# Moving a shared on-chip arena from a start of 32 modulo 128 bytes to a multiple of 128 bytes

## The reference, cut to what matters

```python
# layer 0: 32 query heads of 16, 8 key/value heads, then a residual sum and a layer norm with gamma, beta
x = norm(softmax(q @ k.T / 4 + mask) @ v @ Wo + bo + x) * gamma + beta
# layers 1 and 2: 16 heads of 128 over the same context, one extra key and value (bias_k, bias_v) per head
for i in (1, 2):
    h = layer_norm(x) * scale_i + offset_i
    q, k, v = h @ wq_i + bq_i, ctx @ wk_i + bk_i, ctx @ wv_i + bv_i
    x = x + softmax(q @ [k, bias_k].T / sqrt(128)) @ [v, bias_v] @ wo_i + bo_i
# MLP: width 2048, exact gelu
h = layer_norm(x) * scale + offset
x = x + gelu(h @ w_fc1 + b_fc1) @ w_fc2 + b_fc2
```

## Time and profile before

| what | value |
|---|---|
| time, median of 3 runs | 2512.69 us (2512.53 to 2516.67) |
| the profiled execution: its own time | 2512.67 us |
| its span, first to last instruction | 2510.9 us |
| matmuls busy (PE) | 2395.5 us, 95% of the span |
| weight loads busy (PEld) | 2045.5 us, 81% |
| VectorE, ScalarE, GpSimd busy | 1240.8, 862.7, 807.9 us |
| mean granted TensorE clock | 0.987 |

### The profile page before, as it was taken

One profiled execution on the slowest core, in us unless ns is written; L12 is line 12 of the kernel. 1 busy time (PEld: TensorE's weight loads), 2 busy tenths in 40 slices (PEclk: granted clock), 3 DMA queues, 4 the chain that ended last, 5 costly groups with the idle time before them and its releaser, 6 DMA issues.

```text
span 2510.9 us, 40711 instructions
## 1 busy us (share of the span) xinstructions
PE 2395.5 (95%) x14896; PEld 2045.5 (81%) x14896; DVE 1240.8 (49%) x2038; ACT 862.7 (34%) x2484; POOL 807.9 (32%) x584
## 2 busy tenths in 40 slices
PE   6898999999999999999979889999999999998999
PEld 5677888888888888777766778888888888887777
DVE  6985333434433333465579853333354333334654
ACT  5964222223322222332259642222233222223311
POOL 4964222233322223210059542223243222323100
PEclk9999999999999999999989999999999999999999
DMA  5002001111000101011140020111110010110110
GB/s 200 10 10 80 34 33 58 35 57 56 35 34 33 42 33 54 18 43 58 67 165 10 10 80 34 42 50 42 50 55 34 34 42 33 42 50 14 59 42 34
DMA packets 34545, 120.16 MB, mean 48 GB/s; under 512 B 3456, under 2 KB 3712, under 8 KB 33408
## 3 DMA queue, kind: packets, MB, share of 16 engines
q1 hardware_dynamic: 34432, 118.69, 13.1%
HBM read 114.48 MB, written 4.19 MB: 47 GB/s over the span
## 4 chain that ended last, share of the span: by engine, by line
PE 84%; DVE 6%; issue 4%; ACT 3%; POOL 3%; DMA 0%; DVEq 0%; SPq 0%; ACTq 0%; POOLq 0%
PE PS L504 71%; PE PS L691 4%; PE PS L707 4%; PE PS L699 2%; POOL XN L367 1%; ACT PS L1008 1%; DVE XN L1203 1%; PE PS L572 1%; ACT AT L1008 1%; DVE MX L1208 1%; PE PS L682 1%; DVE X L1227 1%; POOL P0D L367 0%; DVE SUM L1213 0%; DVE XN L1285 0%
## 5 line engine op out<-in xcount | busy, mean ns | idle before, releaser
L504 PE MATMUL PS<-AT,W 128*128 128x512 f32 x2496 | 606.8, 393 | 10.8 <-DVE AT L1295 10.7
L504 PEld LDWEIGHTS PS<-AT,W 128*128 128x128 f32 x2496 | 468.4, 189 | 117.0 <-DVE AT L1295 18.0
L429 POOL TENSOR_TENSOR PR<-PR,RC 128x512 f32<-128x512 f32 x128 | 133.3, 1041 | 984.3 <-DVE RC L1372 984.3
L1227 DVE TENSOR_TENSOR X<-PS,X 128x512 f32<-128x512 f32 x416 | 286.1, 689 | 312.0 <-PE PS L504 306.9
L504 PE MATMUL PS<-CT,W 128*128 128x512 f32 x1584 | 403.3, 404 | 29.8 <-DVE W L334 25.0
L504 PE MATMUL PS<-W,CX 128*128 128x512 f32 x1632 | 403.7, 401 | 7.6 <-DVE Q L1195 3.1
L504 PE MATMUL PS<-W,CT 128*128 128x256 f32 (+1 forms) x3264 | 406.7, 284 | 0.0
L504 PEld LDWEIGHTS PS<-W,CT 128*128 128x128 f32 x3264 | 394.8, 191 | 1.6 <-issue 0.8
L504 PEld LDWEIGHTS PS<-CT,W 128*128 128x128 f32 x1584 | 293.2, 191 | 90.1 <-DVE W L334 25.5
L504 PEld LDWEIGHTS PS<-W,CX 128*128 128x128 f32 x1632 | 300.3, 188 | 80.0 <-DVE Q L1195 4.3
L1039 ACT ACTIVATE CX<-PS,VEC 128x512 fp32r<-128x512 f32 x128 | 88.1, 688 | 672.4 <-PE PS L707 672.4
(11 more groups left out here) (109 smaller groups left out, 2452.0 us busy)
## 6 DMA issues: line engine op xcount, KB each, us to landing
RAW<-in_wq SPq DMA_DIRECT2D x44, 512.0 KB, 4.4
RAW<-in_wo SPq DMA_DIRECT2D x44, 512.0 KB, 3.2
RAW<-in_wk SPq DMA_DIRECT2D x40, 512.0 KB, 3.2
RAW<-in_wv SPq DMA_DIRECT2D x40, 512.0 KB, 3.7
X<-in_x SPq DMA_DIRECT2D x2, 2048.0 KB, 9.0
BVR<-in_bv_rows SPq DMA_DIRECT2D x8, 512.0 KB, 3.8
out<-X SPq DMA_DIRECT2D x4, 1024.0 KB, 4.2
BIASVR<-in_biasv_rows SPq DMA_DIRECT2D x6, 512.0 KB, 5.0
```

The costliest lines, as they stand in the source:

```text
L429: nc.gpsimd.tensor_tensor(PR[:, :, 0:P], PR[:, :, 0:P], RC[:, 0, 0:BT].unsqueeze(2).to_broadcast([P, BT, P]), ALU.mult).then_inc(norm_done, 1)
L504: ins = nc.tensor.matmul(out, lhs(c, a), rhs(c, b), start=(k == 0), stop=(k == total - 1))
L1227: V_.tensor_tensor(X[:, tile, :], PS[:, bank, :], X[:, tile, :], ALU.add).then_inc(done, 1)
```

## The change

```diff
         ARENA = 61440
-        at = (nc.sbuf_base + 31) // 32 * 32
-        sb("arena", [P, ARENA // 4])
+        at = (nc.sbuf_base + 127) // 128 * 128
+        sb("arena", [P, ARENA // 4 + 24])
```

## The result

| | before | changed |
|---|---|---|
| median of 20 runs | 2514.23 us (2512.53 to 2516.67) | 2507.02 us (2503.72 to 2512.64) |
| ratio, 95% interval | | 0.9974 (0.9967 to 0.9981) |
| profiled execution, its span | 2512.67, 2510.9 us | 2507.58, 2505.8 us |
| mean granted clock of the profiled run | 0.987 | 0.985 |

The change makes the kernel 0.26% faster, 7.2 us between the medians and 5.1 us between the two profiled spans. The forecast was no change, 2512.7 us, with 0.15 for faster. The time lies inside the stated range, the direction was missed.

The account below looks back on a forecast made before the run. The prediction took the matrix engine to bound the kernel, with the large products at 71% of the span. Span 2510.9 us plus 1.8 us around it plus 0 for every term gave 2512.7 us, range 2500 to 2518 us.

Parts of the forecast that it names:

- the 0 for the pace of the 512-wide streams out of the arena: Matrix engine, HB and CX streams: the new starts change their pace by nothing, 0 us.
- a price of 17.3 us: HB and CX streams: gain if the residue causes all their slowness, 4.7 us plus 12.6 us; kept as one end.
- Weight loads and transposes show no cost: Matrix engine: loads take 188 ns from the arena, 189 from W; transposes 1.03 us per eight at either residue.
- Keys with both tiles at a multiple of 128 run at two paces: Keys stream, CT moving and W stationary: 237.2 and 228.1 ns at the same addresses, so pace depends on what ran before.
- The 128-wide products run alike in and out of the arena: Attention's small products: 110.5 ns outside the arena, 110.6 and 112.0 inside, so no gain from these 2048 matmuls.
- a nanosecond of a stream in the MLP is one of the kernel: MLP: the matrix engine is busy for all of 100 us, so each nanosecond per matmul counts in the kernel's time.
- Rival A: HB and CX streams: stationary operand at residue 32 or 96 costs, 0 or 64 does not; 17.3 us gain, 2495.4 us, chance 0.14.
- Its variant with 2508.0 us: Only a start at 0 counts, not 64: CX of layers 1 and 2 stays slow, little more than HB's 4.7 us left.
- Rival B: Matrix engine: two operands starting at the same residue get in each other's way; 8.4 us slower, 2521.1 us, chance 0.06.
- VectorE, ScalarE, GpSimd and the transfer were costed at 0: Other engines' arena tiles: 0, bounds -0.3 us and 0; ROWV's transfer: 0, with 128 us of slack.
- The 3 beats: ROWV's transfer: its new address wastes 3 more beats of 32 bytes on 4096 bytes, an estimated 2% of the transfer.

Follow-up runs that it names:

- e1: The kernel before with HB alone moved from residue 32 to 0 modulo 128: 2512.83 us, ratio 0.9997 to the kernel before.
- e2: The kernel before with CX of layers 1 and 2 alone moved by 32 bytes, from residue 96 to 0: 2513.99 us, ratio 1.0006.
- f1: e3 with the whole arena another 128 bytes up: 2509.58 us, ratio 0.9984 to the kernel before.
- f2: e3 with 128 bytes of padding ahead of W, moving W and all behind it: 2519.26 us, ratio 1.0022 to the kernel before.
- f4: e3 with 32 bytes of padding ahead of W and the arena another 32 up: 2519.04 us, ratio 1.0019 to the kernel before.
- h1: e3 plus four PSUM banks for the second MLP product, with AT moved 128 bytes and W and all behind it 256: 2510.64 us, ratio 0.9988 to before.
- e4: The changed kernel with HB put back to residue 32 and CX to 96: 2516.86 us, ratio 1.0014 to the kernel before.
- e3: The changed kernel with PT and CX another 64 bytes up, so every arena tile starts at a multiple of 128: 2506.42 us, ratio 0.9971 to before.

## Why the prediction was wrong

The failing step is the one named in it: the 0 for the pace of the 512-wide streams out of the arena. The rows had shown the two slow streams, 6.1 and 7.7 ns slower, and a price of 17.3 us. The runs showed CX 5.5 ns a matmul faster and 6.4 us in all, and HB 7.3 ns faster while it does not wait. I argued it away with three comparisons, and each was of something else.

- *Weight loads and transposes show no cost.* True, and they still show none: HB's loads take 188 ns before and in e1. But what differs is the step from one pair of load and matmul to the next. The transposes are 128 columns wide and use IDENT as moving tile, so they have another pair of starts.
- *Keys with both tiles at a multiple of 128 run at two paces.* The 237.2 ns hold the first step after a float32 product, 0.31 us. Inside the same stream without it, in a timeline of the kernel before,

```profile
801.58 1.55 PE L504 MATMUL PS<-CT,W 128*128 128x512 f32 x6
```

six take 1.55 us, (1.55 - 0.397) / 5 = 231 ns, and the last step of the twelve is 227 ns: it settles. HB and CX did not settle in 24. I should have compared stretches of equal kind, as I had done for AT. The keys are not fully understood, though: in the changed kernel, with CT and W where they were, the same six take a little less.

```profile
798.69 1.53 PE L504 MATMUL PS<-CT,W 128*128 128x512 f32 x6
```

- *The 128-wide products run alike in and out of the arena.* They do. But width matters: equal starts help the 512-wide streams and cost the 256-wide one 3 ns.

A second step failed beside it: that a nanosecond of a stream in the MLP is one of the kernel. It rested on a window with PE busy for all of 100 us. But recorded matmuls overlap by some 160 ns, so a wait of 0.1 us between two of them leaves PE busy. The group of HB's weight loads showed 15.7 us of waiting for VectorE's X, and with HB alone moved (e1) it shows 17.8 us and no gain in the time. In the same window VectorE is busy for 53%, not for half or less.

Rival A had the place right, of its 12.6 us for CX about half came, and it had the cause wrong: it is not the stationary tile's residue modulo 128 (e2, f1), but its distance from the moving tile modulo 256 (f2, f4, h1). Its variant with 2508.0 us met the time by chance, with the parts exchanged: it let HB gain and CX stay, and the runs show that HB brings little or nothing (e1), while CX's matmuls take 6.4 us less. Rival B had the sign reversed: equal starts are the best case for a 512-wide stream. It named the two tiles together, which was the right pair to look at.

The size comes out so. CX moved from 96 to 192 modulo 256 away from W, and gains 0.12 us per 24 matmuls: 1632 / 24 x 0.12 = 8.2 us at most, since CX0 in layer 0 runs in blocks of six beside other work; its group gave 6.4. A block of the MLP is 0.07 us shorter, some 2 us over the 32 blocks, and e1 shows none of it in the total. The extra time at 1.2 GHz takes a part of this. The profiled execution was 5.1 us shorter and the medians differ by 7.2. No run moved CX alone to a fast distance, so that CX brings the gain rests on its group's time and on e1 and e4, and f1 shows that some 2 us of a total can stay unexplained by the paces. VectorE, ScalarE, GpSimd and the transfer were costed at 0, and their rows agree. The 3 beats that the prediction estimated from the Trainium skill (DMA: Bandwidth & Descriptors, "How a descriptor splits into AXI transactions") had no time to cost: the read of ROWV comes 139 us after the issue. The section speaks of what a transaction reads, and ROWV is the side that is written, so the estimate may not even apply. No run here shows the beats.

## What to carry to other kernels

Where the matrix engine is busy throughout, compare the start-to-start time of streams of the same width, away from their first steps and waits, and treat a difference of a few ns that persists as a cost with a cause. Here it was the distance of the two tiles' starts modulo 256 bytes, which is worth choosing per stream: for fp32r streams with a weight load for each matmul, as here, equal for the 512-wide products and 32 bytes apart for the 256-wide one. Then look at the next wait, since a faster stream behind a fixed chain on another engine gives its gain back, as HB did until it had more banks.

## What the runs showed of the hardware

Start-to-start times of the fp32r streams, by the distance of the stationary from the moving tile's start modulo 256 (512-wide, from rows of six to sixteen matmuls):

| distance | stream and kernel | ns |
|---|---|---|
| 0 | AT (before), CX (f2, f4) | 226.8, 226.7 |
| 32 | AT (f4) | 232.6 |
| 96 | CX (before) | 234.2 |
| 128 | CX (e2, f1), AT (f2, h1), HB (f1) | 232.9, 232.6, 231.6 |
| 160 | HB (before) | 232.6 |
| 192 | CX (changed) | 228.7 |
| 224 | CX (e4) | 232.9 |

The keys (CT moving, W stationary) fit this only roughly: six of them take 1.53 to 1.55 us at distance 0, depending on the kernel, 1.55 at 128 and 1.56 at 32. The 256-wide values stream has 119.9 ns at 0, 116.8 at 224 (W 32 ahead of CT), 117.4 at 192 and 118.5 at 128. A period of 128 is excluded by e2 against e3, and one of 512 by HB in the changed kernel, which is 82176 = 321 x 256 bytes from W and as fast before its wait (226.5 ns) as AT, which is 32768 = 128 x 256 bytes from W. What in the chip does this is not settled. Nor is what moves the short stretches at 1.2 GHz from one passage to another. The float32 products kept their 1.05 to 1.06 us per eight in every kernel. K and Q kept their distance to each other. PT moved by 64 bytes against V in e3 and all kernels made from it, from 192 to 128 modulo 256, without a difference.
